# An earlier load in focal input, and another order of PE's and VectorE's work in focal modulation

## The chip, the cores and the metric

The kernel runs on one core of a Trainium2 chip. The metric is the device time of one execution in microseconds; lower is better. A core has five engines that run their own instruction streams and wait for each other through semaphores: TensorE (PE) for matmuls and transposes, VectorE (DVE), ScalarE (ACT), GpSimd (POOL), and SyncE (SP), which here issues all DMA transfers.

## What is computed

Two layers of a metaformer on x of 32 pictures, 56 x 56 pixels, 128 channels, all in float32. The parts that matter here are the first half of the second layer:

```python
def _L1_conv_ref(x, Wf, bf, k0, k1, k2, Wh, bh, gamma, beta, Wp, bp):
    y = jnp.einsum('bhwc,cd->bhwd', x, Wf) + bf
    q, ctx, gates = y[..., :C], y[..., C:2 * C], y[..., 2 * C:]
    ...                      # three depthwise convolutions of ctx, gated and summed: ctx_all
    modulator = jnp.einsum('bhwc,cd->bhwd', ctx_all, Wh) + bh
    x_out = q * modulator
    x_out = (x_out - mu) * rsqrt(var + 1e-3) * gamma + beta
    return jnp.einsum('bhwc,cd->bhwd', x_out, Wp) + bp

x = x + _L0_conv_ref(_ln_c(x), ...)      # window attention
t = t + _L0_ffn_ref(_ln_t(t), ...)       # mixture of experts
x = x + _L1_conv_ref(_ln_c(x), ...)      # focal modulation
t = t + _L1_ffn_ref(_ln_t(t), ...)       # a recurrence over the 3136 pixels of a picture
```

`_ln_c` and `_ln_t` normalise each pixel over its channels.

## The kernel before

Six stages run one after the other, each with its own buffers and semaphores: attention, experts, focal input, convolution, focal output (modulation), recurrence. Between them everything lies in DRAM.

In every stage the work is cut into steps. The helper run_steps (line 67) calls a function step(n, first, last) for each of them: the first ones and the last ones are written out, those between are a hardware loop. Each engine has its own step function, and the order of the calls in it is the order of the engine's instructions. hold (line 86) is a wait on a semaphore. An engine may be some steps ahead of another: a call with n + 9 in the step of n does its work nine steps ahead. There is no scheduler; the order is as written.

**Focal input** (focal_input_stage, line 998). A picture is 7 steps (NG = 7) of 4 tiles; 32 pictures make 224 steps. xin has two slots, each for a whole picture; load_quads (line 980) loads one with 6 DMAs, for each half 48, 5 and 3 rows of 14336 bytes. In the step of n, DVE takes the statistics of the tiles of n + 11 (layer_stats, line 1185 and the following), then the negated mean of n + 9, then copies the transposed tiles of n + 8 (spread, L1214). POOL and ACT each normalise half the tiles of n + 9 (L1106 and L1134; semaphores normed and normed_act). PE transposes n + 8 and does two matmul groups for n: the query (pq) and context with gates (py). ACT copies these to qs, cs and gs. SP's step (line 1056) has, at the first step of a picture, the wait until that picture is normalised as a whole and the load of the picture two later into the same slot; at the last step of a picture it waits for ACT's copies and stores q (L1068), c (L1070) and the gates (L1075), each from one of two slots.

**Focal output, modulation** (focal_output_stage, line 1573). Again 224 steps. In a step PE does:

- turn_context: four transposes of cin to pt (L1905)
- project: for each of four tiles a 128x129 matmul (L1926) and a 128x1 one (L1927) into pz, one of two slots; needs the residual of two steps before
- modulator: one 448-column matmul into pm, one of two slots (L1912); it waits until gate has read what the slot held
- gram: four matmuls of z with itself (L1933)

A float32 matmul shows as two records. DVE does gate (three operations that multiply the modulator with q, L1801), y_mean, y_mean_square and y_variance (L1808, L1812, L1817), negate (L1853), x_variance (L1846), residual (four operations that read pz, scale it and add it to xin, L1827; semaphore x3_made), x_parts (four BATCH_NORM_STATS2, L1835) and x_statistics (L1841). POOL takes the roots of the variances (L1713) and adds a bias to xin; ACT copies the transposed context to cT (L1737), squares y (L1743) and normalises z (L1752). SP loads cin, q and x of the picture two later and stores x3 step by step.

In the step of n before the change, PE's order is: turn_context(n + 10), project(n + 1), modulator(n + 9), gram_of(n − 3). DVE's is: gate(n + 9), y_mean(n + 1), negate(n − 2), y_mean_square(n + 1), x_variance(n − 1), y_variance(n + 1), residual(n), x_parts(n), x_statistics(n).

Of the kernel before, what the change touches and what calls it, by code (L numbers as in the profile page):

```python
# [66 lines left out]
def run_steps(eng, count, unroll, step, ahead=3):  # L67

    rounds = (count - 1 - ahead) // unroll
    if rounds < 3:
        for n in range(count):
            step(Step(0, unroll, n), n, n - count)
        return
    for n in range(unroll):
        step(Step(0, unroll, n), n, n - count)
    with eng.Fori(1, rounds) as it:
        for u in range(unroll):  # L80
            step(Step(it, unroll, u), MANY, -MANY)
    for n in range(rounds * unroll, count):
        step(Step(0, unroll, n), n, n - count)


def hold(eng, sem, value, ticks):


    eng.wait_ge(sem, value)
    eng.sem_inc(ticks, 1)  # L90
# [889 lines left out]
def load_quads(eng, dst, src, n, sem):  # L980

    for half in range(2):
        for row, real, rows in ((0, SHIFT, 48), (48, SHIFT + 48, 5), (IMG - SHIFT, 0, SHIFT)):
            p0 = half * IMG + real
            eng.dma_start(dst[p0:p0 + rows, :, :].rearrange("p k c -> p (k c)"),
                          dram(src, n.val(PIX * C, (half * IMG + row) * TILES * C), [(TILES * C, rows), (1, TILES * C)]))\
               .then_inc(sem, 16)
# [10 lines left out]
def focal_input_stage(nc, B, x2, Wf, bf, ident, q, c0, gates):  # L998
# [3 lines left out]
    NG = TILES // GRP  # L1002
    N = B * NG
# [5 lines left out]
    with S.ctx:  # L1009
# [38 lines left out]
        @block.sync  # L1048
        def _(sp):
            for dst, src in ((idn[:], ident), (wf[:], Wf), (wlast[:], row_to_all(Wf, OUT, (C - 1) * OUT))):  # L1050
                sp.dma_start(dst, src).then_inc(const_in, 16)
            sp.wait_ge(centred, 1)
            sp.dma_start(wf[C - 1:C, :], dram(bf, 0, [(OUT, 1), (1, OUT)])).then_inc(const_in, 16)

            def step(n, first, last):
                m, c = image(n)
                s = m.slot(2)
                if first == 0:
                    for k in range(2):
                        load_quads(sp, xin[:, k, :, :], x2, m + k, x_in[k])  # L1060
                if c == 0 and last < -2 * NG:
                    hold(sp, normed, n.val(1, NG), ticks)
                    hold(sp, normed_act, n.val(1, NG), ticks)
                    load_quads(sp, xin[:, s, :, :], x2, m + 2, x_in[s])
                if c < NG - 1:
                    return
                hold(sp, q_read, n.val(1, 1), ticks)
                sp.dma_start(dram(q, m.val(PIX), [(B * PIX, C), (1, PIX)]), qs[:, s, :]).then_inc(q_out[s], 16)  # L1068
                hold(sp, c_read, m.val(NG + 1, NG + 1), ticks)
                sp.dma_start(dram(c0, m.val(C * ODD), [(B * C * ODD, P), (1, C * ODD)]),  # L1070
                             cs[:, s, :, :].rearrange("p c j -> p (c j)")).then_inc(c_out[s], 16)
                hold(sp, g_read, m.val(NG + 1, NG + 1), ticks)

                for half, j0 in ((0, 0), (1, 1)):
                    sp.dma_start(dram(gates, m.val(EVEN, half * ROW * 4 * B * EVEN), [(4 * B * EVEN, ROW), (B * EVEN, 4), (1, EVEN)]),  # L1075
                                 gs[(1 - half) * ROW:(2 - half) * ROW, s, :, j0:j0 + EVEN]).then_inc(g_out[s], 16)

            run_steps(sp, N, U, step, 3 * NG)
            for s in range(2):
                images = (B + 1 - s) // 2  # L1080
                sp.wait_ge(c_out[s], 16 * images)
                sp.wait_ge(g_out[s], 32 * images)
                sp.wait_ge(q_out[s], 16 * images)
# [489 lines left out]
def focal_output_stage(nc, B, ctx_all, q, x2, Wh, bh, gamma, beta, Wp, bp, ident, x3, gram):  # L1573
# [11 lines left out]
    with S.ctx:  # L1585
# [142 lines left out]
        @block.scalar  # L1728
        def _(act):
            act.wait_ge(const_in, CONSTS)  # L1730
            act.wait_ge(filled, 6)

            def context_out(n, first):
                hold(act, turned, n.val(1, 1), ticks)
                if first >= 2:
                    hold(act, modulated, n.val(1, -1), ticks)
                act.activation(cT[:, n.slot(2), :], pt[:, 0:COLS8], ACT.Copy).then_inc(cT_out, 1)  # L1737

            def square(n):
                m, c = image(n)  # L1740
                rows = slice(c * ROWS8, (c + 1) * ROWS8)
                hold(act, gated, n.val(1, 1), ticks)
                act.activation(sq[:, m.slot(2), :, :, rows], yT[:, m.slot(2), :, :, rows], ACT.Square).then_inc(squared, 1)  # L1743

            def norm_z(n, first):
                m, c = image(n)
                hold(act, nmean_done, n.val(1, 1), ticks)
                if first >= 2:
                    hold(act, gram_added, n.val(1, -1), ticks)
                b = n.slot(2)  # L1750
                for t in range(GRP):
                    ins = act.activation(z[:, b, t, 0:C], xin[:, m.slot(2), GRP * c + t, :], ACT.Identity,  # L1752
                                         bias=nmean[:, b, t:t + 1], scale=rstd[:, b, GRP + t:GRP + t + 1])
                ins.then_inc(z_normed, 1)

            def step(n, first, last):
                if first == 0:
                    for k in range(10):
                        context_out(n + k, k)
                        if k >= 2:  # L1760
                            square(n + k - 2)
                if last < -10:
                    context_out(n + 10, first + 10)
                if last < -8:
                    square(n + 8)
                if first >= 2:
                    norm_z(n - 2, first - 2)
                if last == -1:
                    norm_z(n - 1, first - 1)
                    norm_z(n, first)  # L1770

            run_steps(act, N, U, step, AHEAD)
            act.wait_ge(gram_added, N)
            act.activation(gout[:], pg[:, 0:C + 1], ACT.Copy).then_inc(gram_copied, 1)

        @block.vector
        def _(dve):
# [53 lines left out]
            def x_parts(n):  # L1831
                m, c = image(n)
                hold(dve, x3_made, n.val(1, 1), ticks)
                for t in range(GRP):
                    ins = dve.bn_stats(stat[:, t, :], xin[:, m.slot(2), GRP * c + t, :])  # L1835
                ins.then_inc(parts, 1)
# [20 lines left out]
            def step(n, first, last):  # L1857
                if first == 0:
                    for k in range(9):
                        gate(n + k, k)  # L1860
                    y_mean(n)
                    y_mean_square(n)
                    y_variance(n).then_inc(varied, 1)
                if last < -9:
                    gate(n + 9, first + 9)
                if last < -1:
                    y_mean(n + 1)
                if first >= 2:
                    negate(n - 2, first - 2)
                if last < -1:  # L1870
                    y_mean_square(n + 1)
                if first >= 1:
                    ins = x_variance(n - 1)
                if last < -1:
                    ins = y_variance(n + 1)
                ins.then_inc(varied, 1)
                residual(n)
                x_parts(n)
                x_statistics(n)
                if last == -1:  # L1880
                    x_variance(n).then_inc(varied, 1)
                    negate(n - 1, first - 1)
                    negate(n, first)
# [4 lines left out]
        def _(pe):  # L1888
# [47 lines left out]

            def step(n, first, last):
                if first == 0:
                    for k in range(10):
                        turn_context(n + k, k)  # L1940
                        if k:
                            modulator(n + k - 1, k - 1)
                    project(n, 0)
                if last < -10:
                    turn_context(n + 10, first + 10)
                if last < -1:
                    project(n + 1, first + 1)
                if last < -9:
                    modulator(n + 9, first + 9)
                if first >= 3:  # L1950
                    gram_of(n - 3, first - 3, last - 3)
                if last == -1:
                    for k in (2, 1, 0):
                        gram_of(n - k, first - k, last - k)
# [405 lines left out]
```

## Time and profile before

| what | value |
|---|---|
| median of 3 runs | 10446.7 us (10440.45 to 10485.31) |
| the profiled execution: its own time | 10452.25 us |
| its span, first to last instruction | 10450.5 us |
| mean granted clock of TensorE | 0.921 of 2.4 GHz |
| focal input | about 4015 to 5080 us of the span |
| modulation | about 6948 to 8575 us of the span |

The two stages that the change touches hold about a quarter of the time. In the profile, a view of stretches gives for each stretch the busy time of every engine with the number of instructions, the granted clock (1.00 is 2.4 GHz, 0.50 is 1.2 GHz) and the mean busy share of the 16 DMA engines. A timeline lists instructions in order, alike ones merged: start, duration of the group, engine, line, operation, out<-in, count, and in brackets the idle time before it with what ended it. The start of the following group tells when the next one could begin, which may be before the end of the group, since instructions overlap in the pipeline.

### The profile page before, as it was taken

The numbers are of one execution on the slowest core, as the hardware profiler recorded it, in microseconds if no ns is written. First come the engines' busy times: TensorE is split into PE (matmuls) and PEld (weight loads), VectorE is DVE, ScalarE is ACT, GpSimd is POOL, SyncE is SP. The second block draws the span as 40 slices with busy tenths as digits, with TensorE's granted clock in tenths as the row PEclk, the third lists the DMA queues.
The fourth block names the chain that finished last, engine by engine and source line by source line (L and its number), as shares of the span: only waits on it lengthen the run. The fifth ranks groups of instructions, "written<-read, shape, count | busy, mean of one in ns | idle before, by whom it ended". The sixth has DMA issues, their size and how long they took to land. (4 is left out here: it accounts for less than half of the span.)

```text
span 10450.5 us, 326086 instructions
## 1 busy us (share of the span) xinstructions
PE 8720.3 (83%) x109727; PEld 5558.7 (53%) x109727; DVE 6436.5 (62%) x21703; ACT 4554.8 (44%) x12677; POOL 5645.2 (54%) x6830
## 2 busy tenths in 40 slices
PE   8999999788888885555499999977777878888888
PEld 6777777333333333444355555546666665555554
DVE  8999999788888885444255555545555542222222
ACT  5666666455555554444333333323333333333333
POOL 8999998677777775444222222224444444444444
PEclk9999999899999998777799999987777769999999
DMA  1222221111111113555444444436556532222222
GB/s 53 58 58 58 58 58 54 52 46 50 46 50 50 46 50 94 158 158 158 151 155 156 146 159 159 158 103 137 130 125 132 135 79 57 56 56 56 56 56 53
DMA packets 798451, 960.01 MB, mean 92 GB/s; under 512 B 323882, under 2 KB 662635, under 8 KB 774380
## 3 DMA queue, kind: packets, MB, share of 16 engines
q1 hardware_dynamic: 798060, 956.25, 32.3%
q14 instruction: 323, 2.65, 0.1%
q8 instruction: 68, 1.11, 0.0%
HBM read 576.90 MB, written 455.45 MB: 99 GB/s over the span
## 5 line engine op out<-in xcount | busy, mean ns | idle before, releaser
L944 PE MATMUL moe_pe_out<-moe_we,moe_xnT 128*128 128x512 f32 x3136 | 1526.0, 621 | 373.0 <-DVE moe_odd L837 196.9
L1544 PE MATMUL conv_pc<-conv_c,conv_toep 128*128 128x432 f32 (+1 forms) x3584 | 1371.0, 535 | 0.0
L741 ACT ACTIVATE moe_scaled<-moe_pe_out,moe_gate 128x128 f32<-128x128 f32 x3136 | 891.8, 367 | 861.1 <-PE moe_pe_out L944 859.2
L944 PEld LDWEIGHTS moe_pe_out<-moe_we,moe_xnT 128*128 128x128 f32 x3136 | 555.9, 194 | 1183.8 <-issue 1182.4
L1406 POOL TENSOR_TENSOR conv_g<-conv_c,conv_gate 128x896 f32<-128x896 f32 x128 | 365.5, 2855 | 1474.8 <-DVE conv_out L1507 1371.0
L2106 ACT ACTIVATE rec_yT<-rec_ph 128x32 f32<-128x32 f32 x3136 | 618.3, 197 | 1242.2 <-PE rec_ph L2227 1242.2
L282 POOL TENSOR_SCALAR att_xn<-att_xin,att_mv,att_rstd 128x128 f32<-128x128 f32 x1024 | 1007.0, 997 | 54.2 <-POOL att_rstd L278 54.2
L2227 PE MATMUL rec_ph<-rec_yT,rec_vt 128*32 128x32 f32 x25080 | 844.8, 207 | 195.7 <-ACT rec_yT L2106 121.0
L1544 PEld LDWEIGHTS conv_pc<-conv_c,conv_toep 128*128 128x128 f32 x3584 | 672.6, 191 | 601.7 <-issue 601.7
L2153 DVE COPY rec_xT<-rec_pin 128x512 f32<-128x512 f32 x196 | 135.6, 692 | 1240.2 <-PE rec_pin L2199 1240.2
L1713 POOL TENSOR_TENSOR mod_rstd<-mod_var,mod_halfneg 112x8 f32<-112x8 f32 x226 | 372.1, 1646 | 943.6 <-DVE mod_var L1817 940.7
L679 POOL TENSOR_TENSOR moe_paired<-moe_scaled 128x256 f32<-128x256 f32 x784 | 569.9, 727 | 530.4 <-ACT moe_scaled L741 515.5
L2227 PEld LDWEIGHTS rec_ph<-rec_yT,rec_vt 128*32 128x32 f32 x25080 | 495.6, 108 | 648.6 <-ACT rec_yT L2106 609.7
L1752 ACT ACTIVATE mod_z<-mod_xin,mod_nmean,mod_rstd 112x128 f32<-112x128 f32 x896 | 368.9, 483 | 1006.3 <-DVE mod_nmean L1853 958.5
L1926 PE MATMUL mod_pz<-mod_wpx,mod_yT 128*112 128x129 f32 x1792 | 475.9, 363 | 315.1 <-DVE mod_xin L1827 315.1
L2258 PE MATMUL rec_p_idle<-rec_idle_x,rec_idle_w 128*32 128x256 bf16 (+1 forms) x9408 | 718.1, 299 | 0.0
L2081 POOL TENSOR_SCALAR rec_xn<-rec_xin,rec_mv,rec_rstd 128x127 f32<-128x127 f32 x784 | 634.0, 821 | 41.5 <-POOL rec_rstd L2078 41.5
L1440 ACT ACTIVATE conv_c<-conv_pc,conv_gap 64x448 f32<-64x448 f32 x512 | 321.9, 629 | 634.6 <-PE conv_pc L1544 629.8
L1801 DVE SCALAR_TENSOR_TENSOR mod_yT<-mod_pm,mod_hcol,mod_qT 128x224 f32<-128x224 f32 (+2 forms) x672 | 238.8, 459 | 579.1 <-PE mod_pm L1912 535.5
L1248 PE MATMUL foc_px<-foc_idn,foc_xn 112*128 112x112 f32 x896 | 147.9, 295 | 457.4 <-POOL foc_xn L1106 438.5
L2076 POOL TENSOR_SCALAR rec_rstd<-rec_mv 128x4 f32<-128x4 f32 x196 | 45.6, 233 | 893.2 <-DVE rec_mv L2148 864.2
L1432 ACT ACTIVATE conv_c<-conv_pc,conv_gap 128x448 f32<-128x448 f32 x512 | 296.4, 630 | 485.3 <-PE conv_pc L1544 485.3
(202 smaller groups left out, 21141.3 us busy)
## 6 DMA issues: line engine op xcount, KB each, us to landing
conv_toep<-rows_dram SPq DMA_DIRECT2D x32, 2304.0 KB, 14.0
c<-foc_cs SPq DMA_DIRECT2D x32, 1856.0 KB, 7.8
conv_cin<-c SPq DMA_DIRECT2D x32, 1856.0 KB, 9.0
ctx_all<-conv_out SPq DMA_DIRECT2D x32, 1792.0 KB, 6.5
att_xin<-x_windows SPq DMA_DIRECT2D x512, 98.0 KB
x<-att_x1s SPq DMA_DIRECT2D x1024, 49.0 KB
moe_xin<-x SPq DMA_DIRECT2D x112, 448.0 KB, 3.5
x<-moe_acc SPq DMA_DIRECT2D x112, 448.0 KB, 2.7
```

Source lines behind the costliest of these rows:

```text
L282: ins = pool.tensor_scalar(xn[:, a, t, :], xin[:, s, t, :], mv[:, a, t, 0:1], rstd[:, a, t:t + 1], ALU.subtract, ALU.mult)
L679: pool.tensor_tensor(paired[:, b, :, :], scaled[:, b, 0:2, :], scaled[:, b, 2:4, :], ALU.add)\
L741: ins = act.activation(scaled[:, b, e, :], pe_out[:, b, 1, e * C:(e + 1) * C], ACT.Identity, scale=g)
L944: ins = pe.matmul(pe_out[:, b, half, :], xnT[:, n.slot(2), t, :], we[:, half * 4:half * 4 + 4, :].rearrange("d e c -> d (e c)"), start=Tru ...
L1544: ins = pe.matmul(pc[k][:, half, 0:HALF * wide].rearrange("p (b i) -> p b i", i=wide)[:, :, i0:i1], w, tile[:, b, i0 + away:i1 + away], st ...
L1713: pool.tensor_tensor(rstd[:, n.slot(2), :], var[:, n.slot(2), :], halfneg[0:TOK, :], ALU.pow).then_inc(rstd_done, 1)
L1752: ins = act.activation(z[:, b, t, 0:C], xin[:, m.slot(2), GRP * c + t, :], ACT.Identity, bias=nmean[:, b, t:t + 1], scale=rstd[:, b, GRP + ...
L1926: pe.matmul(pz[0:TOK, b, t, 0:C + 1], tile_of(yT, m, c, t), wpx[:], start=True, stop=True)
L2081: ins = pool.tensor_scalar(xn[:, a, t, 0:C - 1], xin[:, n.slot(4), t, 0:C - 1], mv[:, a, t, 0:1], rstd[:, a, t:t + 1], ALU.subtract, ALU.mult)
L2106: act.activation(yT[:, a, cs], ph[:, a, cs], ACT.Sigmoid).then_inc(moved, 1)
L2227: ins = pe.matmul(ph[r:r + 32, n.slot(2), cs], vt[:, r:r + 32], before, start=False, stop=True, skip_group_check=True)
L2258: pe.matmul(p_idle[r:r + 32, 0:384 if t >= 2 * SUB else 256], idle_w[:, r:r + 32], idle_x[:, 0:384 if t >= 2 * SUB else 256], start=True, ...
```

## The change

In focal input, SP begins the load of a picture at the fifth step (c == NG − 3) of the picture three before it, ahead of that picture's stores; it was at the first step of the picture two before it, behind the stores of the picture before. It waits for the same event as before, the last norm of the picture that held the slot. The third picture's load stays in the first step. The number of steps written out at the end grows from 3 NG to 4 NG.

In modulation, PE does modulator(n + 10) first in its step, then turn_context(n + 11), project(n + 1), gram_of(n − 3). DVE does residual(n) first and gate(n + 9) after x_parts(n). ACT copies the context of n + 11 instead of n + 10.

```diff
+            def load_freed(m, steps):
+                hold(sp, normed, steps, ticks)
+                hold(sp, normed_act, steps, ticks)
+                load_quads(sp, xin[:, m.slot(2), :, :], x2, m, x_in[m.slot(2)])
...
                 if first == 0:
                     for k in range(2):
                         load_quads(sp, xin[:, k, :, :], x2, m + k, x_in[k])
-                if c == 0 and last < -2 * NG:
-                    hold(sp, normed, n.val(1, NG), ticks)
-                    hold(sp, normed_act, n.val(1, NG), ticks)
-                    load_quads(sp, xin[:, s, :, :], x2, m + 2, x_in[s])
+                    load_freed(m + 2, n.val(1, NG))
+                if c == NG - 3 and last < -2 * NG - 3:
+                    load_freed(m + 3, n.val(1, NG + 3))
                 if c < NG - 1:
                     return
...
-            run_steps(sp, N, U, step, 3 * NG)
+            run_steps(sp, N, U, step, 4 * NG)
... modulation, ACT
-                    for k in range(10):
+                    for k in range(11):
                         context_out(n + k, k)
-                        if k >= 2:
-                            square(n + k - 2)
-                if last < -10:
-                    context_out(n + 10, first + 10)
+                        if k >= 3:
+                            square(n + k - 3)
+                if last < -11:
+                    context_out(n + 11, first + 11)
... modulation, DVE
-                if last < -9:
-                    gate(n + 9, first + 9)
+                residual(n)
                 if last < -1:
                     y_mean(n + 1)
...
                 ins.then_inc(varied, 1)
-                residual(n)
                 x_parts(n)
+                if last < -9:
+                    gate(n + 9, first + 9)
                 x_statistics(n)
... modulation, PE
-                    for k in range(10):
+                    for k in range(11):
                         turn_context(n + k, k)
                         if k:
                             modulator(n + k - 1, k - 1)
                     project(n, 0)
                 if last < -10:
-                    turn_context(n + 10, first + 10)
+                    modulator(n + 10, first + 10)
+                if last < -11:
+                    turn_context(n + 11, first + 11)
                 if last < -1:
                     project(n + 1, first + 1)
-                if last < -9:
-                    modulator(n + 9, first + 9)
```

## Rows read from the trace of the kernel before

**Rows 1.** Stretch: us, busy of PE, PEld, DVE, ACT, POOL, clock, DMA, GB/s; modulation

```profile
7100.00:8400.00 1300.00, 1035.57 (x5534) 876.99 (x5532) 747.11 (x3692) 468.90 (x1109) 531.38 (x369) 0.75 0.59 132
```

**Rows 2.** Waits of DVE, 4100 to 5050: total us, times, longest us

```profile
DVE foc_stat L1185 <- DMA foc_xin<-x: 374.2, 29, 13.4
```

**Rows 3.** Timeline of DVE in focal input: the ends of two stalls

```profile
4501.39 0.87 DVE L1185 BATCH_NORM_STATS2 foc_stat<-foc_xin 112x6 f32<-112x128 f32 x4 [12.92 <-DMA foc_xin<-x]
...
5030.61 0.87 DVE L1185 BATCH_NORM_STATS2 foc_stat<-foc_xin 112x6 f32<-112x128 f32 x4 [13.01 <-DMA foc_xin<-x]
```

**Rows 4.** Timeline of SP's DMA issues, 4484 to 4520

```profile
4484.30 4.90 SPq L985 DMA_DIRECT2D foc_xin<-x  x6
4511.21 0.39 SPq L1068 DMA_DIRECT2D q<-foc_qs  x1
...
4517.91 2.65 SPq L985 DMA_DIRECT2D foc_xin<-x  x3
```

**Rows 5.** Timeline of POOL: the last norm of the older picture

```profile
4505.74 0.90 POOL L1106 TENSOR_SCALAR foc_xn<-foc_xin,foc_rstd,foc_nmean 112x127 f32<-112x127 f32 x2 [0.16 <-DVE foc_nmean L1198]
```

**Rows 6.** Tile mod_mean_y: one per step, ns min/median/max, first and last start

```profile
L1808 DVE COPY mod_mean_y<-mod_pz x224: 140/151/165, 6998.6 to 8562.1; 112x4 f32<-112x4 f32 x112
```

**Rows 7.** Timeline of DVE in modulation, one step at 2.4 GHz

```profile
7647.01 1.08 DVE L1801 SCALAR_TENSOR_TENSOR mod_yT<-mod_pm,mod_hcol,mod_qT 128x224 f32<-128x224 f32 x3 [1.41 <-PE mod_pm L1912]
7647.98 0.16 DVE L1808 COPY mod_mean_y<-mod_pz 112x4 f32<-112x4 f32 x1
...
7648.87 1.13 DVE L1827 SCALAR_TENSOR_TENSOR mod_xin<-mod_pz,mod_rstd,mod_xin 112x128 f32<-112x128 f32 x4
7650.14 0.87 DVE L1835 BATCH_NORM_STATS2 mod_stat<-mod_xin 112x6 f32<-112x128 f32 x4
```

**Rows 8.** Timeline of PE in the same step

```profile
7644.20 0.45 PE L1926 MATMUL mod_pz<-mod_wpx,mod_yT 128*112 128x129 f32 x2 [1.01 <-DVE mod_xin L1827]
...
7645.73 0.27 PE L1927 MATMUL mod_pz<-mod_mean,mod_sq 128*112 128x1 f32 x2
7645.86 1.00 PE L1912 MATMUL mod_pm<-mod_cT,mod_wh 128*128 128x448 f32 x2
7646.70 1.06 PE L1933 MATMUL mod_pg<-mod_z 112*128 112x129 f32 x8
7647.59 0.62 PE L1905 MATMUL mod_pt<-mod_idn,mod_cin 112*128 112x112 f32 x4
```

**Rows 9.** Timeline of PE in modulation, the step before, at 1.2 GHz

```profile
7635.88 0.74 PE L1926 MATMUL mod_pz<-mod_wpx,mod_yT 128*112 128x129 f32 x2 [0.80 <-DVE mod_xin L1827]
...
7639.09 1.84 PE L1912 MATMUL mod_pm<-mod_cT,mod_wh 128*128 128x448 f32 x2
7640.73 1.93 PE L1933 MATMUL mod_pg<-mod_z 112*128 112x129 f32 x8
7642.45 0.75 PE L1905 MATMUL mod_pt<-mod_idn,mod_cin 112*128 112x112 f32 x4
```

**Rows 10.** Third picture's load, nothing ahead: POOL, SP, DVE timelines; its last stretch

```profile
4057.27 0.90 POOL L1106 TENSOR_SCALAR foc_xn<-foc_xin,foc_rstd,foc_nmean 112x127 f32<-112x127 f32 x2 [0.99 <-DVE foc_nmean L1198]
...
4058.34 2.32 SPq L985 DMA_DIRECT2D foc_xin<-x  x6
...
4073.50 0.88 DVE L1185 BATCH_NORM_STATS2 foc_stat<-foc_xin 112x6 f32<-112x128 f32 x4 [0.61 <-DMA foc_xin<-x]
...
4067.00:4073.00 6.00, 5.31 (x36) 4.08 (x34) 5.41 (x22) 5.42 (x13) 5.63 (x11) 1.00 0.18 44
```

**Rows 11.** DMA queue, 4478 to 4510: packets, MB, share of 16 engines

```profile
q1 hardware_dynamic: 992, 5.17, 57.1%
```

**Rows 12.** Tile mod_cin: what PE waited for before the transposes, whole stage

```profile
  DMA mod_cin<-ctx_all: 24.3, 2
```

**Rows 13.** Stretches in modulation before and after a fall of the clock

```profile
7653.60:7656.40 2.80, 0.87 (x9) 0.72 (x8) 2.47 (x13) 2.06 (x6) 1.52 (x1) 1.00 1.23 204
...
7658.94:7662.30 3.36, 3.36 (x12) 2.54 (x13) 1.29 (x6) 0.00 (x0) 0.00 (x0) 0.50 1.05 291
```

## The prediction

> **What bounds the kernel now.** I read the page first (the 40 slices), then one line for each of the two stages that the change touches, then in each stage the waits and one period of its loop, engine by engine.
>
> Focal input runs in a rhythm of one picture. The waits name what it waits for: DVE stood 374.2 us in 29 stalls on the load of xin, 12.9 us each [rows 2]. The reader sees one such stall of 12.92 us end at 4501.39, and the last at 5030.61: 16 periods between them, 33.08 us each [rows 3]. So 33.1 − 12.9 = 20.2 us of a period are work. In SyncE's own order the load (4484.30) lands 17.1 us after its issue starts; the next picture's load starts at 4517.91, behind the stores of q (4511.21), c and the gates [rows 4]. The place that it fills was free long before: GpSimd's last norm of the old picture ended at 4505.74 + 0.90 = 4506.64, 5.25 us after the landing [rows 5]. The load waits 11.3 us for a place in a queue, not for memory.
>
> Modulation is a loop between DVE and PE. 224 steps lie 7.01 us apart on the mean [rows 6], though DVE is busy only 57% of it and PE 80%, at a mean granted clock of 0.75 [rows 1]. One step at 2.4 GHz [rows 7, 8]: residual ends at 7648.87 + 1.13 = 7650.00, PE's project starts 0.14 later; back one step, project starts at 7644.20, modulator at 7645.86 (1.66) and ends 1.00 later, gate starts 0.15 after that, y_mean 0.97 after gate, residual 0.89 after y_mean. 0.14 + 1.66 + 1.00 + 0.15 + 0.97 + 0.89 + 1.13 = 5.94, the distance of the two projects. At 1.2 GHz [rows 9]: project 7639.09 − 7635.88 = 3.21 and modulator 1.84; the same sum is 8.33 (measured 8.32: 7635.88 to 7644.20). A mean clock of 0.75 means half the time at each level; 1/(0.5/5.94 + 0.5/8.33) = 6.93, 0.08 under the mean. So the bound of this stage is the handover loop, and the clock is half of its price.
>
> **Part 1: the load in front of the stores.** Removed: the wait of a load behind q, c and gate stores. Added: two waits on SyncE at the fifth step of a picture, ahead of these stores. Queued behind them are that picture's stores only; q's store came 9.8 us after the landing, the waits pass 5.25 us after it [rows 3 to 5], and then six load issues take 4.9 us [rows 4], so the stores lose about half a microsecond. ACT needs a stored buffer back only two pictures later; cost nothing, and at most that half microsecond if the buffers were short.
>
> What is late next? The load itself. Two slots hold x; the load of picture M+1 needs the last norm of M−1, and in the program order of DVE this comes after the first statistics of M, so after M has landed. New loop: landing, 5.25 us to the last norm, then the load. A load with nothing in front: the norm ended at 4057.27 + 0.90 = 4058.17, DVE got the data at 4073.50, 15.3 us [rows 10]. Sum 20.6 us, the lower bound of the period; it lies just above the 20.2 of work, so the engines stay a little ahead of it. Now the stores of the last picture lie in the queue when the load comes. Bounds: nothing (20.6), or the load is begun only when everything else is through: one picture's transfers keep the 16 engines 57.1% of 32 us = 18.3 us busy [rows 11], with 5.25 of handover 23.5. Between them, the load of before had c and gates right ahead and took 17.1 − 15.2 (its time from issue, 4058.34 to 4073.50) = 1.9 us longer than the free one; with the stores begun a third of a period earlier I take 1.4: period 22.0.
> Gain 29 × (33.08 − 22.0) = 321 us; bounds 29 × 12.5 = 362 and 29 × 9.6 = 278.
>
> The free load's end is thin: from 4067 to 4073 the DMA engines are busy by 0.18 on the mean, though DVE still waits for data at 4073 [rows 10]. The Trainium skill (DMA: Bandwidth & Descriptors, "Why a DMA increments its semaphore by 16 and not by 1") says that a DMA is spread over the largest number of engines up to 16 that divides its row count, the lowest-numbered ones. By that rule the pieces of 5 and 3 rows go to 5 and 3 engines, three engines carry 10 of the rows where most carry 6, and it is these three in which the stores queue; the trace's thin end agrees. Without it the obstruction could be zero and the gain 362; with it 321.
>
> **Part 2: the order of modulation.** Moved on PE: modulator(n+10) comes first in a step, then the four transposes (now n+11), then project and gram. Moved on DVE: residual first, gate after x_parts. Counts of instructions are the same; the start gains one more modulator ahead, about a microsecond, costed at nothing. The transposes need the context one step earlier; PE waited for it twice, at the start only [rows 12], so some steps of 7 us lie in between.
>
> The wait that goes: DVE's gate for the modulator of the same step. The wait that is new: a modulator writes one of two PSUM slots, so modulator(n+10) waits for gate(n+8), which DVE now does last but one in the step before; queued behind it on PE are the transposes and project(n+1), for which y_mean(n+1) waits on DVE. So there is again a closed loop: gate, modulator, transposes, project, y_mean to y_variance, x_parts, gate. Its pieces at 2.4 GHz: 0.14 handover; modulator to next start 0.84; transposes some 0.45 (four of 0.62 in all, overlapping; lower bound 0.40); project to its end 1.80 (7644.20 to 7645.73 + 0.27); 0.15; y_mean to the next operation 0.89; x_parts, whose four starts take about 0.82 of their 0.87 (upper bound 1.02, with the following wait); gate 1.08 [rows 7, 8]. Sum 6.17. At 1.2 GHz [rows 9]: modulator 1.64, transposes 0.75, project 3.21 + 0.14 for its end; sum 8.82. DVE's remaining work, aggregation and residual, 1.7 us, lies beside PE's 3.1. So at either level the new loop is longer than the old: +0.23 and +0.49. Residual leaves the loop (1.13) but x_parts enters it, and the transposes enter too. Gram stays beside DVE.
>
> The clock decides the mix. Before one rise PE had done modulator and gram back to back at 1.2 GHz, from 7639.09 to 7642.45 [rows 9]; the next step ran at 2.4 [rows 8]. Before a fall it had done the transposes and stood still (1.00 in 7653.60:7656.40, PE busy 0.87 of 2.80 us; 0.50 later) [rows 13]. Project, 128x129 matmuls paired with 128x1 ones, had filled the half-clock stretch ahead of the modulator [rows 9], and the clock was still low behind it. In the new order the two dense pieces stand apart: between modulator and gram lie transposes and project, 4.0 us at 1.2 GHz, and behind gram the wait for gate, 1.5 us. The falls stay as they are (gram, gap). So I expect rises to be rarer. Share of time at 2.4 GHz: bounds 0 and 0.5; I take 0.25, because one of the two things that I saw go before a rise is gone and nothing is added.
> Steps: share 0.5: 7.26 + 0.08 = 7.34; 0.25: 7.96 + 0.08 = 8.04; 0: 8.90. Loss over the 213 steps that have a gate: 70, 219 and 403 us.
>
> The Trainium skill (TensorE: Matmul & The Clock Gate, "Part 4: PE-mode transpose") says that a transpose doesn't count as busy PE in the way that a matmul does. No row here singles them out. By that rule the transposes between modulator and project would thin the half-clock stretch further, and the last rival below, share 0, is what the stage would come to.
>
> **Sum.** −321 + 219 = −102 us. The profiled execution took 10452.3 (span 10450.5 and 1.8 around it), the median of the runs is 10446.7. 10446.7 − 102 = **10345 us**.
>
> **Rivals.** (a) The clock mix stays at one half: −321 + 70 = −251, 10196 us. For it: 0.75 over 1300 us is just half and half [rows 1], as if the stage held itself there; against it: the pattern before a rise. (b) The other side: the clock hardly rises any more. Place: PE in modulation; price up to 403 us against 321: +82, 10529 us. It decides where the step passes 7.01 + 321/213 = 8.52, a share under 0.11. For it: at 1.2 GHz the longest dense run is 1.7 us where it was 3.4. (c) The loop isn't longer, since x_parts or transposes hide where I don't see it: steps as before, −321, 10126 us. Against: the chain above is forced by the two PSUM slots. (d) The change doesn't do what it says in focal input: the stores and the load share the engines so that the load lands as late as its old place in the queue allowed, and only modulation's loss is left: +219, 10666 us. Against: between pictures the DMA engines idle 43% of the time [rows 11].
>
> **How the numbers follow.** Forecast (share 0.1 to 0.4) 0.50; (a) 0.21; (b) 0.16; (c) 0.08; (d) 0.02; 0.03 for a surprise on either side. About 0.5% (52 us) is what a measurement of this kernel can tell. The forecast's own range: share 0.4 gives 7.61 (step with the 0.08), +128, and 0.1 gives 8.54, +326; with the load's bounds 10213 to 10495. Faster by over 0.5% needs a share above 0.18: two thirds of the forecast, (a) and (c): 0.62. Within 0.5%: the forecast's slower part and the milder half of (b): 0.24. Slower: 0.14. The range takes in (a) and most of (b): 10180 to 10515.
>
> **What would show it.** Focal input: stalls of DVE on xin of 1 to 3 us in place of 12.9, landings 21 to 23.5 us apart, the load's issue 5.4 us after a landing and ahead of q. Modulation: PE's modulator waits for gate (mod_yT), DVE's y_mean for project (mod_pz), no wait of gate for the modulator; project to project 6.2 us at 2.4 GHz, 8.8 at 1.2 GHz, mean clock near 0.62. Wrong if DVE runs without a wait on PE in modulation, or if the clock there stays at 0.75.

## The result, and the profile after

The changed kernel takes 10367.1 us (median of 5 runs, 10345.9 to 10402.5) against 10445.3 for the kernel before beside it: ratio 0.992, 95% interval 0.9892 to 0.9948. That is 78 us less, 24 fewer than forecast. The profiled execution has a span of 10368.5 us and a mean clock of 0.910 (lines below L1052 are numbered five higher than before).

**Focal input.** The view of stretches (columns as in [rows 1]) over 400 us in its middle, and modulation's stretch for comparison with [rows 1]:

```profile
4150.00:4550.00 400.00, 335.96 (x2072) 253.07 (x2072) 318.17 (x1571) 333.82 (x767) 314.56 (x580) 1.00 0.90 269
...
7100.00:8400.00 1300.00, 979.41 (x4588) 813.80 (x4586) 607.37 (x3049) 405.92 (x918) 438.11 (x305) 0.63 0.48 106
```

DVE's wait for the load, the answer to [rows 2], over 4150 to 4600:

```profile
DVE foc_stat L1190 <- DMA foc_xin<-x: 15.0, 18, 1.5
```

Two such stalls in DVE's timeline, the answer to [rows 3]:

```profile
4315.59 0.87 DVE L1190 BATCH_NORM_STATS2 foc_stat<-foc_xin 112x6 f32<-112x128 f32 x4 [0.68 <-DMA foc_xin<-x]
4354.45 0.87 DVE L1190 BATCH_NORM_STATS2 foc_stat<-foc_xin 112x6 f32<-112x128 f32 x4 [1.48 <-DMA foc_xin<-x]
```

SP's issues, the answer to [rows 4]:

```profile
4321.06 2.65 SPq L985 DMA_DIRECT2D foc_xin<-x  x6
4324.60 0.39 SPq L1073 DMA_DIRECT2D q<-foc_qs  x1
...
4339.89 2.23 SPq L985 DMA_DIRECT2D foc_xin<-x  x5
```

And the tile view of foc_xin: SP sets an address for each of the six DMAs in each picture of the hardware loop, 24 pictures; first and last start:

```profile
L985 SPq MOVE foc_xin<-x x144: 29/29/29, 4128.0 to 4574.5; - x144
```

The load now comes 5.47 us after a landing (4315.59 to 4321.06) and 3.5 us ahead of q. Over 23 periods a picture takes (4574.5 − 4128.0)/23 = 19.4 us where it took 33.08 (two expectations below say 19.1, which is low by 0.3); DVE waits 0.8 us in a stall instead of 12.9. 29 periods give −397 us.

**Modulation.** One start per step, the answer to [rows 6]:

```profile
L1813 DVE COPY mod_mean_y<-mod_pz x224: 148/161/164, 6613.8 to 8476.9; 112x4 f32<-112x4 f32 x112
```

1863.1 us for 223 steps, 8.35 each, where it was 7.01: +300 us. The waits of 6650 to 8400 (us, times, longest), of DVE and then of PE:

```profile
DVE mod_mean_y L1813 <- PE mod_pz L1932: 801.5, 194, 4.9
DVE mod_xin L1832 <- issue: 94.1, 12, 9.0
```

```profile
PE mod_pm L1917 <- DVE mod_yT L1806: 426.0, 205, 6.8
```

The wait of gate for the modulator is gone; modulator waits for gate and y_mean for project. One turn of that loop on PE, at 1.2 GHz (granted clock 0.50 from 7404.72 to 7413.5), and DVE's part of it:

```profile
7404.72 1.83 PE L1917 MATMUL mod_pm<-mod_cT,mod_wh 128*128 128x448 f32 x2 [2.24 <-DVE mod_yT L1806]
7406.35 0.95 PE L1910 MATMUL mod_pt<-mod_idn,mod_cin 112*128 112x112 f32 x4
...
7410.21 2.07 PE L1938 MATMUL mod_pg<-mod_z 112*128 112x129 f32 x8
7413.59 1.83 PE L1917 MATMUL mod_pm<-mod_cT,mod_wh 128*128 128x448 f32 x2 [1.32 <-DVE mod_yT L1806]
```

```profile
7410.50 0.16 DVE L1813 COPY mod_mean_y<-mod_pz 112x4 f32<-112x4 f32 x1 [4.77 <-PE mod_pz L1932]
...
7412.16 1.04 DVE L1806 SCALAR_TENSOR_TENSOR mod_yT<-mod_pm,mod_hcol,mod_qT 128x224 f32<-128x224 f32 x3
```

The reader sees the loop: modulator at 7404.72, transposes, project up to where gram starts (7410.21), y_mean at 7410.50, gate from 7412.16 to 7413.20, and the next modulator only 0.39 us later; 8.87 us in all.

A hardware loop runs its body, here 14 steps, and jumps back to its start. At each of its 12 jumps DVE stands still, for 6.8 to 9.0 us, and the waits name nothing that it waits for. The first of these stops, and the row of the DMA queue that carries instructions, over 6844 to 6852:

```profile
6844.48 0.36 DVE L1846 BATCH_NORM_AGGREGATE mod_mv<-mod_stat 112x2 f32<-112x6 f32 x4
6851.85 1.12 DVE L1832 SCALAR_TENSOR_TENSOR mod_xin<-mod_pz,mod_rstd,mod_xin 112x128 f32<-112x128 f32 x4 [7.01 <-issue]
```

```profile
q14 instruction: 1, 0.01, 0.6%
```

Each of the 12 stops has one such transfer in it, some 3 us before DVE goes on, while over the stage they stand 23 us apart on the mean (81 in 1830 us). That DVE waits for its own code to be loaded is the nearest reading; no run tests it.

### The profile page after: what moved, and what is told of

Read it like the earlier page. It is cut to its first block and busy times, and to the rows that moved or that the text cites. A ratio compares the mean times of both kernels' runs of the same rounds, so it can differ in the third digit from the quotient of the medians.

```text
span 10368.5 us, 326078 instructions
## 1 busy us (share of the span) xinstructions
PE 8856.6 (85%) x109727; PEld 5638.9 (54%) x109727; DVE 6420.2 (62%) x21703; ACT 4582.3 (44%) x12677; POOL 5643.9 (54%) x6830
## 3 DMA queue, kind: packets, MB, share of 16 engines
q14 instruction: 324, 2.65, 0.1%
## 5 line engine op out<-in xcount | busy, mean ns | idle before, releaser
L1917 PE MATMUL mod_pm<-mod_cT,mod_wh 128*128 128x448 f32 x448 | 392.1, 977 | 446.9 <-DVE mod_yT L1806 446.9
L1931 PE MATMUL mod_pz<-mod_wpx,mod_yT 128*112 128x129 f32 x1792 | 560.7, 413 | 0.0
L1813 DVE COPY mod_mean_y<-mod_pz 112x4 f32<-112x4 f32 x224 | 36.1, 161 | 844.1 <-PE mod_pz L1932 844.1
```

The lines of the kernel that those rows point to most:

```text
L1917: pe.matmul(pm[:, n.slot(2), 0:COLS8], wh[:], cT[:, n.slot(2), :], start=True, stop=True).then_inc(modulated, 1)
L1931: pe.matmul(pz[0:TOK, b, t, 0:C + 1], tile_of(yT, m, c, t), wpx[:], start=True, stop=True)
```

## Each part by itself

**e1_focal_only** keeps the edits in focal input and leaves modulation as before; **e2_mod_only** does the reverse.

> The first part of the change alone: focal input as changed, modulation as before. Theory (the two parts add up): the changed kernel's modulation stage takes 1863 us between its first and last y_mean against 1564 before, 300 us more, so of the total of -78 us some -378 us belong to focal input; this kernel runs 10445 - 378 = 10067 us. Rival (the terms as predicted, -321): 10124 us. Rival (focal input's gain is partly handed back in the next stage): above 10124 us.

> The second part of the change alone: modulation as changed, focal input as before. Theory: 10445 + 300 = 10745 us, granted clock in modulation near 0.61, steps 8.35 us apart. Rival (the clock in modulation is low only because of what the faster focal input leaves behind): below 10650 us, clock 0.7 or more.

Here and below, a ratio is to the kernel before, run beside the variant, and a difference in us is to the changed kernel's 10367.1 unless the text says otherwise. Measured beside a kernel before of 10469.1 us, and with differences to that: e1 10051.3 us, ratio 0.9597 (0.9563 to 0.963), −418 us; e2 10764.9 us, 1.0278 (1.0242 to 1.0314), +296 us. The parts add up to −122, together they brought −78; but the kernel before ran from 10444 to 10502 us in this group, and against the 10445.3 of the other comparison the parts give −394 and +320, −74. So the change is a large gain and a large loss. Modulation in e1 stands at clock 0.75 as before (7.06 us a step), in e2 8.35 us a step: neither part alters the other's stage.

## Modulation: what lengthens the step, and what moves the clock

**e3_swap_holds.** PE's modulator has two waits. In the changed kernel the one for gate, which comes last, stands before the one that has long been met:

```diff
             def modulator(n, first):
+                hold(pe, cT_out, n.val(1, 1), ticks)
                 if first >= 2:
                     hold(pe, gated, n.val(1, -1), ticks)
-                hold(pe, cT_out, n.val(1, 1), ticks)
```

> The changed kernel with the two waits of modulator on PE in the other order: first for cT, then for gate. Theory: gate's end to the modulator's start takes 0.39 us in the changed kernel where other handovers take 0.14, because a second wait and its counter stand between the gate's semaphore and the matmul; the swap gives back about 0.25 us in each of 213 steps, 53 us: 10314 us. Rival (the 0.25 us is the weight load of the modulator, now exposed): no change, 10367 us, the handover stays at 0.39.

Measured 10104.0 us, ratio 0.966 (0.9621 to 0.97), −264 against the changed kernel where −53 was expected. Gate on DVE, then the modulator on PE, then the stretch, in the changed kernel and here:

```profile
7404.13 1.05 DVE L1806 SCALAR_TENSOR_TENSOR mod_yT<-mod_pm,mod_hcol,mod_qT 128x224 f32<-128x224 f32 x3
```

```profile
7405.32 0.99 PE L1917 MATMUL mod_pm<-mod_cT,mod_wh 128*128 128x448 f32 x2 [2.36 <-DVE mod_yT L1806]
```

```profile
6800.00:7500.00 700.00, 524.95 (x2468) 435.98 (x2466) 329.27 (x1655) 219.40 (x496) 237.87 (x166) 0.63 0.48 107
...
6800.00:7500.00 700.00, 478.55 (x2850) 396.79 (x2850) 378.87 (x1902) 252.51 (x571) 274.04 (x191) 0.82 0.58 127
```

The handover is 0.14 us again (7405.18 to 7405.32): the second wait, with what belongs to it, costs 0.25 us when it stands behind the wait that ends late. That is the 53 us. The other 211 came with the clock, 0.82 where the changed kernel has 0.63 over the same stretch: a loop shorter by 0.25 us let PE run at 2.4 GHz for 0.64 of the time in place of 0.26. My pricing, a loop times a fixed mix, missed that. The difference isn't one from run to run: e2, e8 and e11 have the changed kernel's modulation, and over 7100 to 8400 their clock is 0.63, 0.62 and 0.62.

**e7_dense_pair** tests the prediction's clock argument: gram directly behind modulator, so that the pair seen before a rise is back.

```diff
                 if last < -10:
                     modulator(n + 10, first + 10)
+                if first >= 3:
+                    gram_of(n - 3, first - 3, last - 3)
                 if last < -11:
                     turn_context(n + 11, first + 11)
                 if last < -1:
                     project(n + 1, first + 1)
-                if first >= 3:
-                    gram_of(n - 3, first - 3, last - 3)
```

> The changed kernel with gram moved on PE right behind the modulator, ahead of transposes and project: work is added to the loop of one step (0.89 us at 2.4 GHz, 1.72 at 1.2), so its two step times should be 6.26 + 0.89 = 7.15 us and 9.22 + 1.72 = 10.94 us. Theory (the clock rises after modulator and gram back to back): the time share at 2.4 GHz goes from a quarter back to a half, mean clock 0.75, steps 8.65 us, 64 us more than the changed kernel: 10430 us. Rival (the neighbourhood of the two does not matter): clock stays at 0.62, steps 9.6 us, 10640 us.

Measured 10747.6 us, ratio 1.0289 (1.0267 to 1.0311), and PE with the stretch:

```profile
7404.24 1.83 PE L1917 MATMUL mod_pm<-mod_cT,mod_wh 128*128 128x448 f32 x2 [3.60 <-DVE mod_yT L1806]
7405.87 1.93 PE L1938 MATMUL mod_pg<-mod_z 112*128 112x129 f32 x8
7407.59 0.95 PE L1910 MATMUL mod_pt<-mod_idn,mod_cin 112*128 112x112 f32 x4
...
7414.03 1.83 PE L1917 MATMUL mod_pm<-mod_cT,mod_wh 128*128 128x448 f32 x2 [3.25 <-DVE mod_yT L1806]
```

```profile
6800.00:7500.00 700.00, 469.75 (x2051) 409.38 (x2052) 271.73 (x1364) 180.45 (x408) 196.34 (x137) 0.59 0.41 92
```

The pair stands back to back and the clock is 0.59, lower than without it. Gram now lies inside the loop, and PE waits 3.3 to 3.6 us for gate instead of 1.3 to 2.2. Both expectations, 10430 and 10640 us, were too low. The pair is thus not enough to bring the clock back; since this edit also lengthens the loop, it doesn't show that the pair has no effect. e3, at 0.82 without the pair, shows that it isn't needed.

**e9_gram_twice** changes neither the loop nor the order; it fills PE's wait with work, doing gram's four matmuls twice. Its result is then twice too large.

```diff
-                for t in range(GRP):
-                    ins = pe.matmul(pg[:, 0:C + 1], z[:, n.slot(2), t, 0:C], z[:, n.slot(2), t, :],
+                for t in range(2 * GRP):
+                    ins = pe.matmul(pg[:, 0:C + 1], z[:, n.slot(2), t % GRP, 0:C], z[:, n.slot(2), t % GRP, :],
```

> The kernel after the change, but PE does the four gram matmuls of a step twice (gram then counts every row twice; nothing else is changed). The second set stands where PE waits for gate anyway: that wait is 2.2 to 2.6 us in a step that ends at 2.4 GHz and 1.3 us in one at 1.2 GHz, the set costs 0.9 us at 2.4 GHz and 1.7 at 1.2. Theory A (the clock follows how much of the time PE works, whatever the order of the pieces: busy 0.75 of the time at clock 0.63 after the change, 0.91 at 0.93 with project first): the added work raises the clock, the steps shrink towards 6.4 us, and more work makes the kernel faster: 9950 to 10150 us. Theory B (the clock follows something else, the mix stays at 0.62): a slow step is 0.4 us longer, a fast one as before, +60 us: 10430 us.

Measured 9981.3 us, ratio 0.9549 (0.9533 to 0.9565): 386 us less than the changed kernel, with more work. The stretch, and one step on PE:

```profile
6800.00:7500.00 700.00, 529.71 (x3855) 471.25 (x3855) 403.20 (x2026) 268.52 (x607) 290.94 (x202) 0.94 0.60 133
```

```profile
7001.15 1.09 PE L1917 MATMUL mod_pm<-mod_cT,mod_wh 128*128 128x448 f32 x2
...
7004.13 2.03 PE L1938 MATMUL mod_pg<-mod_z 112*128 112x129 f32 x16
7007.58 0.99 PE L1917 MATMUL mod_pm<-mod_cT,mod_wh 128*128 128x448 f32 x2 [1.42 <-DVE mod_yT L1806]
```

GpSimd, with two instructions a step, has 202 of them against the changed kernel's 166 in the same 700 us, at clock 0.94 against 0.63. The second set ends (7004.13 + 2.03) before PE has stopped waiting for gate, so it costs nothing, and the step (7001.15 to 7007.58: 6.43) is near the 6.17 + 0.25 = 6.42 that the forecast's pieces at 2.4 GHz and the longer handover give. What Theory A foretold came: with the loop unchanged, more work in PE's wait raised the clock of this stage.

Two things stay open. The second gram also makes the unbroken run of matmuls behind project longer, and no run tells the added work from the longer run. And how much PE is busy or waits doesn't by itself give the clock: over this stretch it is busy 0.75 of the time at 0.63 in the changed kernel, 0.68 at 0.82 in e3, 0.67 at 0.59 in e7 and 0.76 at 0.94 here. Part of the busy time is the lower clock itself, since the same matmuls then take longer.

**e10_jump_28** has 28 steps in one pass of the loop instead of 14:

```diff
-    U = 2 * NG
+    U = 4 * NG
...
-            return Step(n.loop, 2, n.off // NG), n.off % NG
+            return Step(n.loop, 4, n.off // NG), n.off % NG
```

> The kernel after the change with 28 steps of modulation in one pass of the hardware loop instead of 14, so that every engine jumps back half as often (7 jumps instead of 15 or so). If the jump is what stops DVE for 6.7 us before L1832 every 14 steps, and it shows as steps of 11 to 13 us where the neighbours take 8 to 9.2, the stage gets 8 x 3 = 24 us shorter, steps of 11 to 13 us come every 28 steps: 10343 us. If the stop has another cause (the picture's end, every 7 or 14 steps), the long steps stay at every 14 and the time at 10367 us.

Measured 10343.5 us, ratio 0.9906 (0.9887 to 0.9925), 24 less than the changed kernel. Such medians scatter by more; the stage itself shows it better:

```profile
L1813 DVE COPY mod_mean_y<-mod_pz x224: 149/161/165, 6608.0 to 8455.4; 112x4 f32<-112x4 f32 x112
```

1847.4 us against 1863.1: 16 us less, where e2, e8 and e11 with the same modulation have 1861.0, 1864.6 and 1871.3. By run_steps the loop jumps back 12 times with 14 steps to a pass and 5 times with 28. The 12 steps of over 9.8 us in the changed kernel stand at its 12 jumps, the 3 that are left here at three of the 5, and none stands where a jump was taken out. DVE's waits without a releaser (us, times, longest), over 6650 to 8400:

```profile
DVE mod_xin L1832 <- issue: 28.6, 6, 6.6
```

It was 94.1 us in 12. Five of the six are stops of 4.4 to 6.6 us at the five jumps. So the long steps come from the jump. The expected total was met (10343), but with 24 us where the stage shows 16. The clock did not rise with it: 0.60 over 7100 to 8400 where it was 0.63.

## Focal input: what bounds the period now

**e8_q_twice** stores q a second time, to another tensor, directly behind the first:

```diff
+                sp.dma_start(dram(q_again, m.val(PIX), [(B * PIX, C), (1, PIX)]), qs[:, s, :]).then_inc(q_out[s], 16)
```

> The changed kernel with q stored twice in focal input, the second time to a spare array; 1.57 MB more per picture, issued right behind the first. The changed kernel's periods there are 19.1 us at a DMA share of 0.89. Theory A (the load is served beside the stores and DMA has little room left): the extra 4 to 5 us of transfers push the period above 21 us. Theory B (the loop of landing, last norm and load is the bound, the stores run in its shadow): the period stays at 19 to 20 us.

A single run took 10369.5 us, and the tile view:

```profile
L985 SPq MOVE foc_xin<-x x144: 29/29/29, 4128.1 to 4577.4; - x144
```

(4577.4 − 4128.1)/23 = 19.53 us a period, 0.12 more, though the DMA engines are busy by 0.97 over 4150 to 4550 instead of 0.90. The stores do lie in the shadow of the loop of landing, norm and load.

**e11_whole_rows** loads each half of a picture with one DMA of 56 rows, not rotated:

```diff
+    for half in range(2):
+        eng.dma_start(dst[half * IMG:(half + 1) * IMG, :, :].rearrange("p k c -> p (k c)"),
+                      dram(src, n.val(PIX * C, half * IMG * TILES * C), [(TILES * C, IMG), (1, TILES * C)]))\
+           .then_inc(sem, 16)
...
-                load_quads(sp, xin[:, m.slot(2), :, :], x2, m, x_in[m.slot(2)])
+                load_whole(sp, xin[:, m.slot(2), :, :], x2, m, x_in[m.slot(2)])
```

> The kernel after the change, with focal input's load of a picture as 2 DMAs of 56 rows instead of 6 of 48, 5 and 3 (the rows are then not rotated by three, so the output isn't the reference's). Each row has 14336 bytes as before. Theory A (the landing is set by the engines that carry most rows: with 48, 5 and 3 rows three engines carry 10 rows and the load takes 13.2 us, with 56 rows the fullest carries 8): the load lands in about 11 us, the wait of DVE on xin goes, the period falls from 19.1 to the engines' own work, 18.2 us or somewhat more, 10340 us. Theory B (the landing is set by the whole traffic or by a fixed part, not by the fullest engines): 13 us and a period of 19.1 as before, 10367 us.

A single run took 10340.3 us, 27 less than the changed kernel:

```profile
L992 SPq MOVE foc_xin<-x x48: 29/29/29, 4116.7 to 4539.8; - x48
```

(4539.8 − 4116.7)/23 = 18.40 us a period, and between 4150 and 4600 DVE no longer waits for the load at all. The same bytes in another split land sooner, so the traffic as a whole was not the bound: 48, 5 and 3 cost one microsecond of each period.

Two readings are left. One is the fullest DMA engines, which foretold it; for it, the DMA engines are busy by 0.18 at the end of a load with nothing beside it [rows 10], and 0.18 of 16 engines is 2.9. The other is that there are two DMAs instead of six: SP issues them in 0.9 us instead of 2.65, and each may have a cost of its own. At the start of the stage, with no stores in the queue, the first picture's data come 16.3 us after the first issue in the changed kernel (4024.0 to 4040.28) and 10.7 us in e11 (4022.3 to 4033.03); these 5.6 us are more than the 1.7 us of issuing, but a cost per DMA isn't excluded. The Trainium skill's rule that a DMA goes to the largest number of engines up to 16 that divides its row count (DMA: Bandwidth & Descriptors, "Why a DMA increments its semaphore by 16 and not by 1") is what gave the expectation; the trace agrees with it and does not single it out.

## Versions that beat both

Since the loop is closed by modulator, transposes and project standing behind the wait for gate, either side can open it. **e6_project_first** moves project in front of them on PE; **e5_gate_first** moves gate to the head of DVE's step instead; **e4_two_loops** does both.

```diff
+                if last < -1:
+                    project(n + 1, first + 1)
                 if last < -10:
                     modulator(n + 10, first + 10)
                 if last < -11:
                     turn_context(n + 11, first + 11)
-                if last < -1:
-                    project(n + 1, first + 1)
```

```diff
+                if last < -9:
+                    gate(n + 9, first + 9)
                 residual(n)
...
                 x_parts(n)
-                if last < -9:
-                    gate(n + 9, first + 9)
```

> Focal input as changed; in modulation the modulator stays one step further ahead and gate goes first on DVE, before residual, and on PE project goes before modulator and transposes. Theory (the closed loop over one step is the bound): now project(n+1) needs only residual(n-1) and modulator(n+10) only gate(n+8), each with a whole step between, so both loops close over two steps; the bound is then DVE's own work, 4.5 to 4.7 us a step, or PE's (3.9 us at 2.4 GHz): 214 x (8.35 - 4.7) = 780 us less than the changed kernel, about 9590 us, PE clock above 0.9. Rival (DMA takes over: one picture's transfers of this stage keep the 16 engines busy 0.58 of 50 us, and they are issued in order): steps of 5.5 to 6.5 us, 9760 to 9970 us. Rival (the loop is not the bound): within 100 us of e1_focal_only.

> The changed kernel with only DVE's order edited: gate(n+9) before residual(n), PE's order as changed. Theory (the closed loop over one step is made by both orders together): gate(n+8) now runs near the start of DVE's step before, so modulator(n+10) does not wait for it and the loop closes over two steps; steps near 4.6 us as in e4_two_loops, 9520 to 9600 us. Rival (PE's order alone makes the loop): steps above 6 us, above 9850 us.

> The changed kernel with only PE's order edited: project(n+1) before modulator(n+10) and the transposes, DVE's order as changed. Theory: project waits only for residual(n-1) and no longer stands behind a modulator that waits for gate; the loop closes over two steps, 9520 to 9600 us. Rival (gate's late place on DVE is what costs): steps above 6 us, above 9850 us.

Measured: e4 9516.0 us, ratio 0.9084 (0.9052 to 0.9115); e5 9607.8, 0.919 (0.9174 to 0.9205); e6 9512.1, 0.9096 (0.9081 to 0.9112). So the edit on PE alone gives all that both give together. The stretches of e5 and of e6:

```profile
6800.00:7500.00 700.00, 620.72 (x4160) 538.42 (x4160) 544.14 (x2766) 355.94 (x829) 398.33 (x277) 0.87 0.81 182
```

```profile
6800.00:7500.00 700.00, 636.31 (x4558) 560.25 (x4557) 594.00 (x3044) 388.84 (x912) 440.88 (x307) 0.93 0.90 200
```

e6 needs 4.54 us a step: the clock is at 0.93, DVE is busy 85% of the time and the DMA engines 90%. e5 was above its 9520 to 9600 by 8 us and e6 below by 8, e4 was 74 under its 9590. e5 needs 5.03 us a step; project still stands behind the modulator there, and PE still waits for gate at times (46.9 us over 6850 to 7550, 13.3 in e6). That this is the difference isn't tested.

**e12_project_first_28** adds e10's edit to e6.

> Project first on PE (9512 us) and 28 steps in one pass of modulation's loop. The first step of each picture takes 5 to 8 us there where the others take 3.9 to 4.4, 3 to 4 us too much in 32 pictures. If the jump causes the half of them, 8 jumps fewer give 8 x 3 = 24 us: 9488 us. If all of them come from the loads of the next picture (the DMA engines are busy by 0.90), nothing changes: 9512 us.

Measured 9537.9 us, ratio 0.9137 (0.9113 to 0.9161): 26 us slower than e6, where 24 faster or nothing was expected. Both kernels have steps of 7 to 8.5 us, and e12 has four of about 10 besides. In the longest PE waits for a load of the context:

```profile
7147.71 0.62 PE L1910 MATMUL mod_pt<-mod_idn,mod_cin 112*128 112x112 f32 x2 [4.17 <-DMA mod_cin<-ctx_all]
```

Over the stage these waits are 20.5 us against 8.9 in e6. At 4.5 us a step, with the DMA engines busy by 0.90, the transfers are likely the next bound, and fewer jumps brought nothing; why the loads land later in e12 I don't know.

## Why the prediction was right or wrong

**The sum** was −321 + 219 = −102; the traces give −397 + 300 = −97 for the two stages, and −82 between the spans. The total was close by luck: two errors of some 80 us have opposite signs.

**Part 1, mechanism right, one term wrong.** The next bound is the loop of landing, last norm and load, as forecast, and no loss by the later stores is to be seen. The 5.25 us from landing to load measured 5.47. The load itself was the mis-sized term: 15.3 + 1.4 for queued stores, measured 19.4 − 5.5 = 13.9. The period fell below what I called its lower bound, 20.6, and the gain of 397 us above what I called its upper bound, 362. That bound rested on a single load, the third picture's, with nothing ahead of it [rows 10]. It was no stray: in the changed kernel the third picture's load again takes 15.2 us (4067.27 to 4082.50). Why a load by itself takes longer than those in a full queue stays open. The 1.4 for the stores was too much: doubling q's store added 0.12 (e8). That the split into 48, 5 and 3 rows has a part in it was right (e11); that it acts through the stores in three engines is not shown. And the 20.2 us of "work" in a period of 33 was no floor either: with the clock at 1.00 over 4150 to 4550, where it was 0.80 before, the engines manage 18.4 (e11).

**Part 2, the loop.** Its pieces hold: in the turn from 7404.72, modulator 1.63 (forecast 1.64), project to y_mean with the transposes 4.15 (0.75 + 3.35 + 0.15 = 4.25), y_mean to gate 1.66 (0.89 + 0.82), gate 1.04 (1.08). Wrong was the handover: I took 0.14 from the residual's handover to project; this one carries a second wait behind the late one and costs 0.39. Missed altogether was the jump of the hardware loop on DVE; before, DVE stood at its gate for the modulator anyway, and most of the stop lay in that wait: gate has nine waits without a releaser, 26.0 us in all and 3.0 at most, and no step is longer than 8.7 us. The one is worth 0.25 a step; the other by estimate 12/7 of what e10 gained by 7 jumps fewer, 27/223 = 0.12. With the pieces a little shorter than forecast that is about the way from 8.04 to 8.35.

**Part 2, the clock.** The share of 0.25 came, 0.26 by the 0.63 over 1300 us, but by luck. e3 is the loop as I had priced it, with 0.14 of handover: its share is 0.64 and its step 7.16 us, shorter than the 7.34 of rival (a), where I had 0.25 and 8.04. The share of 0.25 belongs to a loop that is 0.25 us longer than mine. The argument was wrong too: the pair of modulator and gram doesn't bring the clock back (e7) and isn't needed for it (e3). The value that I chose between 0 and 0.5 was a guess.

The transposes between modulator and project don't hold the share at 0 either: it is 0.26 with them, and 0.88 in e9 with the same transposes. The Trainium skill (TensorE: Matmul & The Clock Gate, "Part 4: PE-mode transpose") says that a transpose doesn't count as busy PE as a matmul does; that this would keep the share at 0, as the prediction read it, the traces don't bear out.

What the runs show instead is a feedback: a higher clock shortens PE's part of the loop (project 1.66 us against 3.21 [rows 8, 9]), and a small change in the loop moves the clock. 0.25 us less in each turn moved it by 0.19 (e3), work that filled the wait by 0.31 (e9). It isn't a rule by which the mean wait gives the clock. PE's waits for gate are 2.1 us on the mean in the changed kernel (426.0/205) and 2.2 in e3 (471.1/210, over 6630 to 8180) at the higher clock, and e10, with fewer stops, stayed at 0.60. What the clock goes by in a step like this stays open.

**The rivals.** (a), the clock at 0.75, and (c), steps as before, did not come, but with one line moved (e3) the steps are 7.16 us long and the kernel takes 10104, below the 10196 of (a). (b) is what e7 comes nearest to, at 0.59. (d), no gain in focal input, is refuted by e1.

## What to carry to other kernels

When a wait is moved, draw the new closed loop through everything queued behind it in program order, and then ask for the order in which no engine has another's critical work queued behind a late wait: here that was worth 855 us more than the change itself (e6 against the changed kernel). Put the wait that ends last directly in front of its instruction. A step that alternates between the two clock levels isn't worth its length times a fixed mix; look for waits on PE first: in this stage the clock rose when they were shortened or filled, which a price at a fixed mix doesn't hold.

## What the hardware showed that I had not expected

- More matmuls, less time: gram done twice brought the stage's clock from 0.63 to 0.94 and the kernel from 10367.1 to 9981.3 us (with a gram that is twice too large).
- A wait that is already met is not free behind one that ends late: 0.39 against 0.14 us from gate to modulator.
- A hardware loop's jump stops DVE for 6.8 to 9.0 us at 14 steps to a pass, with one transfer in the queue of instructions in every stop. Before the change most of it was hidden in another wait.
- With two DMAs of 56 rows instead of six of 48, 5 and 3, the same bytes took a microsecond less of each period, at DMA engines busy by 0.87 instead of 0.90.
